# VectorE takes the last unit's probability sums, group norm's second heads are split anew, ScalarE reads three output tiles and GpSimd one projection low part

## What is computed

```python
a1 = softmax(q1 @ k1.T / scale); a2 = softmax(q2 @ k2.T / scale)
o = (a1 - lam * a2) @ v
y = group_norm(o, 4 groups) * gn_w + gn_b; y = y @ out_w.T + out_b
```

## Time and profile before

| | |
|---|---|
| median of 3 runs | 6028.48 us |
| profiled execution | 6026.64 us |
| its span, first to last instruction | 6024.8 us |
| mean granted TensorE clock | 0.998 of full speed |
| TensorE busy (matmul / weight load) | 5811.1 us, 96% / 3753.6 us, 62% |
| VectorE busy | 4646.9 us, 77% |
| ScalarE busy | 3239.9 us, 54% |
| GpSimd busy | 3092.1 us, 51% |

### The profile page before, as it was taken

One profiled execution on the slowest core, in us unless ns is written; L12 is line 12 of the kernel. 1 busy time (PEld: TensorE's weight loads), 2 busy tenths in 40 slices (PEclk: granted clock), 3 DMA queues, 4 the chain that ended last, 5 costly groups with the idle time before them and its releaser, 6 DMA issues.

```text
span 6024.8 us, 119971 instructions
## 1 busy us (share of the span) xinstructions
PE 5811.1 (96%) x41392; PEld 3753.6 (62%) x41392; DVE 4646.9 (77%) x6567; ACT 3239.9 (54%) x5836; POOL 3092.1 (51%) x1382
## 2 busy tenths in 40 slices
PE   6999999999999999999999999999999999999999
PEld 4566565655656556575665756657566575665656
DVE  5878778687786877878778787787877878777786
ACT  4645546455564655646556465564655646555464
POOL 3826638175380744808447083571835728266282
PEclk9999999999999999999999999999999999999999
DMA  2212222122222222222222221222212222122221
GB/s 77 59 48 61 59 55 53 58 54 59 51 53 61 52 59 54 48 61 58 57 54 48 64 58 55 54 51 61 59 51 56 50 63 59 48 60 50 64 59 47
DMA packets 148810, 338.12 MB, mean 56 GB/s; under 512 B 38625, under 2 KB 61281, under 8 KB 139745
## 3 DMA queue, kind: packets, MB, share of 16 engines
q1 hardware_dynamic: 146656, 329.33, 22.2%
q10 hardware_dynamic: 1536, 1.05, 0.1%
HBM read 90.49 MB, written 17.30 MB: 18 GB/s over the span
## 4 chain that ended last, share of the span: by engine, by line
PE 76%; DVE 10%; issue 7%; ACT 2%; POOL 2%; DMA 2%; DVEq 0%; SPq 0%; ACTq 0%; POOLq 0%
PE psum L1066 18%; PE psum L1285 16%; PE psum L1210 14%; PE psum L1231 13%; PE psum L1374 7%; DVE minus_max L792 6%; PE psum L1238 4%; POOL prob_sums L393 2%; PE psum L1216 1%; PE psum L1118 1%; PE psum L1329 1%; DMA prob_sums<-combine_rows_dram 1%; ACT probs L537 1%; DVE small L707 1%; PE psum L1131 0%
## 5 line engine op out<-in xcount | busy, mean ns | idle before, releaser
L393 POOL TENSOR_TENSOR prob_sums<-probs 128x1024 f32<-128x1024 f32 x752 | 1795.8, 2389 | 2768.5 <-ACT probs L537 2436.3
L537 ACT ACTIVATE probs<-psum 128x512 f32<-128x512 f32 x4096 | 2214.1, 595 | 1317.0 <-PE psum L1285 1282.6
L792 DVE TENSOR_REDUCE minus_max<-psum 128x1 f32<-128x1024 f32 x2048 | 2398.0, 1209 | 363.2 <-PE psum L1210 360.3
L1285 PE MATMUL psum<-stack 98*128 98x512 f32 x4096 | 1408.0, 428 | 3.6 <-DVE max_rows L802 3.6
L393 POOL TENSOR_TENSOR prob_sums<-prob_sums,probs 128x1024 f32<-128x1024 f32 x512 | 1219.1, 2381 | 46.0 <-ACT probs L537 8.3
L1210 PE MATMUL psum<-stack 96*128 96x512 f32 x4096 | 1190.2, 402 | 20.8 <-DVE minus_max L792 18.3
L1231 PE MATMUL psum<-probs,v_tokens 128*32 128x256 f32 x16384 | 1111.0, 385 | 5.9 <-ACT probs L537 5.9
L1285 PEld LDWEIGHTS psum<-stack 98*128 98x128 f32 x4096 | 690.0, 188 | 530.0 <-issue 230.5
L1210 PEld LDWEIGHTS psum<-stack 96*128 96x128 f32 x4096 | 737.7, 188 | 263.9 <-DVE max_rows L802 61.5
L1231 PEld LDWEIGHTS psum<-probs,v_tokens 128*32 128x32 f32 x16384 | 420.8, 109 | 485.8 <-issue 263.4
L1066 PE MATMUL psum<-act_hi,w_hi 128*128 128x512 f32 x1730 | 691.2, 400 | 12.4 <-DVE act_lo L771 10.9
(11 more groups left out here) (156 smaller groups left out, 4672.9 us busy)
## 6 DMA issues: line engine op xcount, KB each, us to landing
stack<-stage SPq DMA_DIRECT2D x1024, 128.0 KB, 3.0
stack<-stage SPq DMA_DIRECT2D x256, 256.0 KB, 3.1
prob_sums<-combine_rows_dram SPq DMA_DIRECT2D x128, 256.0 KB, 4.0
stage<-combine_rows_dram SPq DMA_DIRECT2D x128, 256.0 KB, 3.3
x_tile<-x_dram SPq DMA_DIRECT2D x34, 512.0 KB, 3.5
x_tile<-o_head SPq DMA_DIRECT2D x480, 32.0 KB, 1.9
stack<-max_rows SPq DMA_DIRECT2D x512, 4.0 KB
y_dram<-residual SPq DMA_DIRECT2D x16, 512.0 KB, 2.8
```

The costliest lines, as they stand in the source:

```text
L393: nc.gpsimd.tensor_tensor(total, first, probs[:, k % NP, :], ALU.add).then_inc(sum_pool, 1)
L537: nc.scalar.activation(probs[:, k % NP, half * HALF:(half + 1) * HALF], ps[:, exp_bank(k) + half, :], ACT.Exp).then_inc(p_ready, 1)
L792: v.tensor_reduce(nm[:, u % 2, q:q + 1], flat_in, AX.X, ALU.max, negate=True).then_inc(ring_free, 1)
L1285: mm(ps[:, exp_bank(k) + half, :], stack[0:KS, s, 1, kt * P:(kt + 1) * P], stack[0:KS, s, 0, half * HALF:(half + 1) * HALF], start=True, s ...
```

## The change

1. In unit 15 VectorE does the four adds of 128x1024 (`last_sum`), with a semaphore of its own; ScalarE and TensorE wait for that one there. The first add stands after VectorE's pair 0, the second after pair 1, the third after pair 2 (behind both reciprocals of unit 14), the fourth at tile 6, ahead of head 6's product. GpSimd keeps only the adding of head 6.
2. After the last tile the first half of unit 15's reciprocals stands before `norm_rest(0)` and no longer behind it.
3. Second heads: VectorE writes the first half into `xh` and ScalarE the first half into `on_sb`; for the second half it is as before. VectorE's `norm_low(0, 1)` now stands behind the wait for head 7's DMAs and its own first normalisation. TensorE takes the high product of the second heads' first half before the low product of the first heads' second half.
4. ScalarE reads output tiles 0, 2 and 3, VectorE tile 1 only. The second half of the token transposes waits for ScalarE alone.
5. K2's second half: ScalarE copies it with its bias into `probs` buffer 3 (`k2_part`), GpSimd subtracts the high part for the low part. TensorE's values wait for the copy, SyncE's load and ScalarE's exponential of tile 3 for GpSimd's subtraction.

```diff
-ADDED = [u * NT + kt for u in range(UNITS) for group in sum_groups(u) for kt in group[1:]]
+ADDED = [u * NT + kt for u in range(UNITS - 1) for group in sum_groups(u) for kt in group[1:]]
+LAST_ADDED = [kt for group in sum_groups(UNITS - 1) for kt in group[1:]]
...
+        k2_part = probs[:, NP - 1, 0:HALF]
...
-                            sp.wait_ge(k2_low, b * NH + NH)
+                            sp.wait_ge(k2_low, b + 1)
+                            sp.wait_ge(k2_rest, b + 1)
                         sp.dma_start(*k_parts[2]).then_inc(stack_in[s], 16)
...
+                pool.wait_ge(k2_raw, b + 1)
+                pool.wait_ge(proj_hi, b * PROJ_STEPS + 8)
+                nc.gpsimd.tensor_tensor(stage[:, 1, 3, HALF:N].bitcast(F32R), k2_part, stage[:, 0, 3, HALF:N],
+                                        ALU.subtract).then_inc(k2_rest, 1)
...
-                for u in range(UNITS):
+                for u in range(UNITS - 1):
                     for g, group in enumerate(sum_groups(u)):
...
+                add_head(HEADS - 2)
...
+                nc.scalar.activation(k2_part, ps[:, 5, :], ACT.Identity, bias=vec(V_K2B)).then_inc(k2_raw, 1)
                 for k in range(4):
                     copy_values(k)
...
+                            if k - NP >= (UNITS - 1) * NT:
+
+                                act.wait_ge(sum_dve, b * len(LAST_ADDED) + last_adds(kt - NP))
+                        if k == NP - 1:
+                            act.wait_ge(k2_rest, b + 1)
...
-                for half in range(NH):
-                    norm_heads(1, half, xh).then_inc(on_hi, 1)
-                for half in range(NH):
-                    act.wait_ge(y1_full, b * 4 + 2 * half + 1)
-                    nc.scalar.activation(res[:, 0, half * HALF:(half + 1) * HALF], ps[:, 2 * half, :], ACT.Identity,
-                                         bias=vec(V_OUTB)).then_inc(y1_act, 1)
+                norm_heads(1, 0, on_sb).then_inc(on_first, 1)
+                norm_heads(1, 1, xh).then_inc(on_hi, 1)
+                for k in (0, 2, 3):
+                    act.wait_ge(y1_full, b * 4 + k + 1)
+                    nc.scalar.activation(res[:, k % 2, k // 2 * HALF:(k // 2 + 1) * HALF], ps[:, k, :], ACT.Identity,
+                                         bias=vec(V_OUTB + k % 2)).then_inc(y1_act, 1)
...
+                    if u == UNITS - 1 and kt == NT - 2:
+                        last_sum(1, 5)
...
+                def last_sum(g, kt):
+
+                    u, group = UNITS - 1, sum_groups(UNITS - 1)[g]
+                    n, k = u * GROUPS + g, u * NT + kt
+                    total = psums[:, n % NS, :]
+                    dve.wait_ge(p_ready, b * 2 * UNITS * NT + 2 * k + 2)
+                    if kt == group[1]:
+                        dve.wait_ge(ones_done, b * UNITS * GROUPS + n - NS + 1)
+                    else:
+                        dve.wait_ge(sum_dve, b * len(LAST_ADDED) + last_adds(kt) - 1)
+                    first = probs[:, (k - 1) % NP, :] if kt == group[1] else total
+                    v.tensor_tensor(total, first, probs[:, k % NP, :], ALU.add).then_inc(sum_dve, 1)
...
                 for item in BEFORE:
                     ring_step(item)
                     if item == ("proj", 2):
-                        k2_low_part(0)
-                    if item == ("score", 0, 0):
-                        k2_low_part(1)
+                        k2_low_part()
...
+                        if u == UNITS - 1:
+                            for g, at in (((0, 1),), ((0, 2),), ((1, 4),), ())[pair]:
+                                last_sum(g, at)
                 norm_variance(0)
 
+                sum_recips(UNITS - 1, 0)
                 norm_rest(0)
-                for part in range(RECIPS):
-                    sum_recips(UNITS - 1, part)
+                sum_recips(UNITS - 1, 1)
                 head_out(UNITS - 1)
...
-                norm_low(0, 1)
                 for s in range(2):
                     dve.wait_ge(o_in[s], (b + 1) * (HEADS // 2) * 4 * 16)
...
+                norm_by_dve(0, xh).then_inc(on_hi_dve, 1)
+                norm_low(0, 1)
+                dve.wait_ge(on_hi_dve, b + 1)
+                norm_low(1, 0)
+                norm_by_dve(1, on_sb).then_inc(on_ready, 1)
+                dve.wait_ge(on_ready, b + 1)
+                norm_low(1, 1)
+                dve.wait_ge(y1_full, b * 4 + 2)
+                v.tensor_scalar(res[:, 1, 0:HALF], ps[:, 1, :], vec(V_OUTB + 1), None, ALU.add).then_inc(y1_dve, 1)
...
-                        pe.wait_ge(y1_act, n * 2 + tt // 4 + 1)
-                        pe.wait_ge(y1_dve, n * 2 + tt // 4 + 1)
+                        pe.wait_ge(y1_act, n * 3 + (1, 3)[tt // 4])
+                        pe.wait_ge(y1_dve, n + 1)
...
-                        pe.wait_ge(k2_low, b * NH + tt // 2 - 1)
+                        pe.wait_ge(k2_low if tt == 4 else k2_raw, b + 1)
...
-                for half in range(NH):
-                    project_out(0, half, True)
-                for half in range(NH):
-                    project_out(1, half, False)
-                    project_out(1, half, True)
+                project_out(0, 0, True)
+                project_out(1, 0, False)
+                project_out(0, 1, True)
+                project_out(1, 0, True)
+                project_out(1, 1, False)
+                project_out(1, 1, True)
```

More of the change, by code:

```diff
@@ L70, in adds, with last_adds @@
     u, kt = divmod(tile, NT)
+    if u == UNITS - 1:
+        return len(ADDED)
     upto = max([kt] + [group[1] for group in sum_groups(u) if kt == group[0]])
     return sum(at <= u * NT + upto for at in ADDED)
+def last_adds(kt):
+    upto = max([kt] + [group[1] for group in sum_groups(UNITS - 1) if kt == group[0]])
+    return sum(at <= upto for at in LAST_ADDED)
 def ones_after(u, pair):
@@ L225, in build @@
         proj_hi, k2_full, k2_low = sem("proj_hi"), sem("k2_filled"), sem("k2_low")
+        k2_raw, k2_rest = sem("k2_raw_copied"), sem("k2_low_by_pool")
         stack_in = [sem(f"stack_in{s}") for s in range(NST)]
@@ L329, in batch @@
                     if t == 0:
-                        sp.wait_ge(on_hi, b * NH * CT + NH)
+                        sp.wait_ge(on_hi, b * 3 + NH)
                     else:
@@ L874, in norm_low @@
                     cols = slice(half * HALF, (half + 1) * HALF)
-                    dve.wait_ge(on_hi, b * NH * CT + NH * t + half + 1)
+                    if (t, half) == (1, 0):
+                        dve.wait_ge(on_first, b + 1)
+                    else:
+                        dve.wait_ge(on_hi, b * 3 + NH * t + half + 1 - t)
                     v.tensor_tensor(xl[:, t, cols], on_sb[:, t, cols], xh[:, t, cols],
@@ L1242, in add_up @@
                 def add_up(u, g):
-                    pe.wait_ge(sum_pool, b * len(ADDED) + adds(u * NT + sum_groups(u)[g][-1]))
+                    if u == UNITS - 1:
+                        pe.wait_ge(sum_dve, b * len(LAST_ADDED) + last_adds(sum_groups(u)[g][-1]))
+                    else:
+                        pe.wait_ge(sum_pool, b * len(ADDED) + adds(u * NT + sum_groups(u)[g][-1]))
                     ones_mm(u, psums[:, (u * GROUPS + g) % NS, :], g == len(sum_groups(u)) - 1).then_inc(ones_done, 1)
@@ L1308, in layer_norm @@
                     tokens(b)
[L1309 to L1310 removed]
+                    pe.wait_ge(y1_act, b * 3 + 3)
                     conv_vk(b + 1)
@@ L1322, in project_out @@
                 def project_out(kt, half, low):
-                    pe.wait_ge(on_lo if low else on_hi, b * NH * CT + NH * kt + half + 1)
+                    if low:
+                        pe.wait_ge(on_lo, b * NH * CT + NH * kt + half + 1)
+                    elif (kt, half) == (1, 0):
+                        pe.wait_ge(on_hi_dve, b + 1)
+                    else:
+                        pe.wait_ge(on_hi, b * 3 + NH * kt + half + 1 - kt)
                     cols = slice(half * HALF, (half + 1) * HALF)
```

26 lines of the change are left out of this document (11 added, 15 removed).

## The result

| | median us | lowest to highest | runs |
|---|---|---|---|
| before | 6027.93 | 6027.04 to 6028.73 | 4 |
| after | 5992.25 | 5987.00 to 5992.63 | 4 |

After over before is 0.994, 95% interval 0.9927 to 0.9952: 35.7 us less, where 20 were forecast and the range ended at 29 (5999). The profiled execution took 5991.94 us with a span of 5990.2. All of it is one gain repeated: the token statistics end every 369.16 us instead of 371.51 (first to twelfth batch, (4408.65 - 347.89) / 11 against (4435.67 - 349.08) / 11), 2.35 us per batch where 1.25 were forecast. To the sixteenth batch it is 2.24 per batch, about the 35.7 over 16: in the fifteenth, a late landing costs the changed kernel more than the kernel before (see e4).

The account below looks back on a forecast made before the run. TensorE bounds steady units, so gains lie only where the chain leaves it, twice per batch: 0.5 + 0.5 + 0.25 = 1.25 us, 16 times, 20 us, giving 6008.5 us; range 5999 to 6024.

Parts of the forecast that it names:

- Front: Start of a batch: K2's low part leaves VectorE, so its eight maxima end 0.5 us sooner per batch (0.3 to 0.65).
- Last unit: Unit 15: adds of 1.21 us on VectorE make head 7 ready 1.5 us earlier, first coefficients only 0.45.
- Second heads: After head 7's DMAs: second heads start 0.5 us earlier per batch, 0.93 less 0.4 for transfers meeting.
- the rival without a collision: Head 7's small transfer and the x tile don't meet: second heads gain 0.93 us, total 6001.5 us; chance 0.20.
- the price of the collision: Delay of head 7's small transfer by the next x tile's load: 0.4 us taken, between 0 and 1.2.
- Behind them: From the second heads to the end of the token statistics: 0.25 us less per batch (0 to 0.4).
- The transfers don't meet: Head 7's landing stays 2.1 us beside the x tile: 1.68 us per batch gained, 6001.5 us; chance 0.20.
- the forecast's own sign: Landing time of ScalarE's head 7 transfers, 2.1, 2.5 or 3.3 us, was to choose between the first three cases.
- The front gives nothing: TensorE's values or unit 1's operands set the turn: only 0.75 us per batch gained, 6016.5 us; chance 0.06.
- The adds cost on VectorE what they cost on GpSimd: Last-unit adds take 2.38 us each, second heads start 3.4 late: slower, 6070 us, deciding from about 1.6; chance 0.07.
- The small transfer waits for the x tile: Head 7's transfer lands behind the x tile, second heads 0.2 us later than before: 6019.5 us; chance 0.25.

Follow-up runs that it names:

- e4: The changed kernel with one wait more: ScalarE issues head 7's last two DMAs only when the first heads are complete; 6050.76 us.
- e3: The changed kernel with the last unit's four adds back on GpSimd, all else kept; 6020.01 us.
- e7: The changed kernel with VectorE's last-unit adds of tiles 1 and 4 made twice; 6018.18 us.
- e6: e4 with SyncE also holding the next x tile's load until head 7 has landed; 5998.75 us.
- e8: The changed kernel with the old split of the second heads and of the output tiles; 5993.7 us.
- e1: The kernel before with only K2's second low half changed, to ScalarE's copy and GpSimd's subtraction; 6020.15 us.
- e10: The changed kernel with the add of tile 7 of unit 14 on VectorE too; 5980.58 us.

## Why the prediction was wrong

**Front**: right. 0.5 forecast, 0.44 measured; GpSimd's subtraction took 1.28 us as estimated.

**Last unit**: right in nearly every step. Adds of 1.15 and 1.23 for 1.21; the last exponential no longer waits; the last ones-product at 332.89, 332.25 in before's time, goes without waiting; head 7 ready at 336.33 in before's time, for 336.5; first coefficients 0.67 earlier, for 0.45. The first two adds took 1.97 and 1.52, held by GpSimd; the first ended at 324.86 in before's time all the same, for 325.0. One step was wrong and bound nothing: GpSimd's add for head 6 was put behind VectorE's product at tile 7, but that product is head 7's first softmax, and GpSimd makes its add straight behind its last sum (324.38). In the kernel before only its place in GpSimd's program made it late.

**Second heads**: here the forecast failed, at the step "ScalarE is in order: four first-head operations start 0.45 earlier and end at 337.7, its two DMA issues end at 339.0, and only then comes the second root". The step took the issue at 338.01 to stand behind the four operations. What it followed was head 7's readiness, at 337.98 (337.56 + 0.42). The last of the four ran to 338.15, so even the kernel before had the issue inside it, by 0.14 us:

```profile
337.35 0.80 ACT L548 ACTIVATE act_hi<-x_tile,small 128x512 fp32r<-128x512 f32 x1
```

What is said of the kernel before, that every engine works its own instructions in the order written, needs this limit: ScalarE's issue comes in its turn, but not only after the arithmetic ahead of it is done.

The issues therefore moved with head 7, by 1.6 us (14.10 to 12.47) and not by 0.45; in e3 and e7, where both come later, the first issue again starts inside the third operation. Four things follow:

- The x tile doesn't catch up with them. It follows the second issue by 1.1 us (337.65, 338.76), as it did before (338.7, 339.77). The collision doesn't happen, and of the landing 0.3 us are added for a reason that stays open. What the forecast feared is e4.
- The second root isn't behind the issues. At 339.30 it waited for VectorE (L884), and the coefficients were there at 340.24, 339.6 in before's time, for 340.0; the second variance, put at 339.1, was ready at 338.6.
- The second heads start 1.63 earlier (17.52 to 15.89) and not 0.5. Even the rival without a collision had only 0.93.
- The misplaced issue cost the forecast most by what it let it fear. Of the 1.13 us missing, 0.43 were the price of the collision. Another 0.41 lie between the 0.93 and e6, where the issues do stand behind the first heads and nothing collides (second heads at 16.18): first heads and landing both came a little earlier than worked out. Only 0.29 are what the earlier issue is worth by itself (16.18 to 15.89).

The Trainium skill, page "Perfetto Trace Analysis", section "Per-instruction lifecycle: what the profiler-reported window actually captures", describes what the fence of ScalarE shows: an arithmetic instruction of ScalarE is pushed to a queue of the engine and the sequencer turns to the next instruction, while a DMA is issued by the sequencer itself. The trace agrees (337.00 inside 336.60 to 337.40).

**Behind them**: right, 0.25 forecast, 0.26 measured (e8).

**The sum**: 0.44 + 1.63 + 0.25 = 2.3 us per batch, against 0.5 + 0.5 + 0.25. Times 16 it is 37 us, for 35.7 measured; the late landing in the fifteenth batch takes 1.7 us back. Two terms were right to 0.06, the third was short by 1.1. The range missed because its best case for that term, 0.93, was itself bounded by the misplaced issue and 0.7 short. That "faster" came true owes something to luck: had ScalarE's issues stood where the forecast had them, the kernel would have been e4, 23 us slower than before.

**The rivals.** None decided. "The transfers don't meet" was right in that they don't, and its 6001.5 still 9 us too high. The landing of 2.4 would by the forecast's own sign (2.1, 2.5 or 3.3) have chosen the forecast, so that sign misleads. "The front gives nothing" is refuted by e1. "The adds cost on VectorE what they cost on GpSimd" had the place right, and e7 its slope: 2.4 us more cost 1.82, so there is some slack, as forecast; only the gain to be used up was larger. "The small transfer waits for the x tile" is real in e4: there it costs 58 us against the changed kernel, 3.7 a batch, where the forecast's worst was 1.2. It was too low for the landing (the second small transfer took 1.5 more), and it left out that TensorE's clock falls behind such a wait (0.50 after 3.99 us). The one landing of 3.8 that spoke for this rival was not its work.

What is late next: the landing and VectorE's second coefficients, in 8 batches of 16 each.

## What to carry to other kernels

Before a DMA issue is counted as behind its engine's arithmetic, look whether the trace has one that starts inside an operation ahead of it, and ask which semaphore its start follows. Where a small transfer ends a serial chain, keep the large ones that a shorter chain sets free at a microsecond's distance behind it, and count the wait they could cause at TensorE's lower clock. A late landing that comes in single batches can be a load of instructions; look at the other DMA queues too. GpSimd's adds on a critical path are worth moving to a VectorE that is idle there, even though the two hold each other up.

## What the runs showed of the hardware that was not expected

- ScalarE's DMA issue isn't held by its running operations: 337.00 and 337.65, inside operations of 336.60 and 337.31 that stand ahead of it. With a wait for their result (e4) the first came 1.13 later (13.60 for 12.47).
- VectorE's adds and GpSimd's hold each other up, in both directions, and the profile counts the waiting as duration. VectorE's 323.53 took 1.97 us and not 1.15, and ended 1.1 after GpSimd's 322.04 + 2.39 = 324.43. GpSimd's head add, begun at 324.38, took 1.71 and not 0.73, and ended (326.09) 0.6 after VectorE's (325.50). VectorE's next took 1.52 and not 1.23. In e10, where it starts 0.3 ahead of VectorE's add, the head add took 0.74.
- After 3.99 us of idle TensorE the granted clock was 0.50, 1.2 GHz, over the next 4 us (e4, 1462 to 1466). In the changed kernel, with gaps of 1.0 to 1.1, it stayed at 1.00 in the row shown, and the statistics end 7.4 after the second heads in each of those 15 batches; behind the one gap of 1.91, in a batch with a late landing, it was 0.63 and 0.52 in the next two stretches of 2 us. In e4's median batch the second heads came 2.0 later and 1.5 more went through the clock.
- Two transfers of 32 KB landed after 1.9 us with nothing issued near them (e6), after 2.1 to 2.4 with 512 KB issued 0.94 behind the second (2.1 before and in e3, 2.4 after), and with the 512 KB issued between them after 1.85 for the first and 3.64, at most 4.64, for the second (e4).
- A load of instructions can hold a small transfer, by the times of their packets; no run removes one. All landings of ScalarE's transfers over 2.9 us outside e4 have a 16 KB load of queue q8 at that moment, with the small transfer's last packets starting as it ends (before, after, e1, e10: batch 15; e6: batch 4).
